# An attention loop on one core: the row of reciprocals goes through the shared PSUM bank ahead of the value products, and the shift is made by a two-scalar operation

## The reference

```python
def _L0_attn_ref(hidden_size, Wq_c, bq_c, Wq_up, bq_up, Wkv_c, bkv_c, Wkv_up, bkv_up, Wo, bo):
    ...
    scores = jnp.einsum('bhqd,bhkd->bhqk', q, k) / np.sqrt(Q_HEAD)
    attn = jax.nn.softmax(scores, axis=-1)
    o = jnp.einsum('bhqk,bhkv->bhqv', attn, v)
    out = jnp.einsum('bhsv,Hv->bsH', o, Wo) + bo
    return out
...
x = x + _L0_attn_ref(_layernorm(x, axis=-1), ...)
x = x + _L0_ffn_ref(_layernorm(x, axis=-1), ...)
```

## Time and profile before

| | |
|---|---|
| median of 3 runs | 1855.05 us |
| the profiled execution | 1852.05 us, its span 1850.2 us |
| PE busy | 1650.0 us, 89% |
| DVE busy | 1618.4 us, 87% |
| ACT busy | 1416.3 us, 77% |
| POOL busy | 969.6 us, 52% |
| granted TensorE clock | 0.994 of full speed |

### The profile page before, as it was taken

One profiled execution on the slowest core, in us unless ns is written; L12 is line 12 of the kernel. 1 busy time (PEld: TensorE's weight loads), 2 busy tenths in 40 slices (PEclk: granted clock), 3 DMA queues, 4 the chain that ended last, 5 costly groups with the idle time before them and its releaser, 6 DMA issues. The chain is left out here.

```text
span 1850.2 us, 23339 instructions
## 1 busy us (share of the span) xinstructions
PE 1650.0 (89%) x7316; PEld 753.7 (41%) x7316; DVE 1618.4 (87%) x2088; ACT 1416.3 (77%) x1979; POOL 969.6 (52%) x1355
## 2 busy tenths in 40 slices
PE   7988988998989889889989898898898988988799
PEld 6733333333333333333333333333333333333344
DVE  6679999999989999999989999999989999999565
ACT  5578888888878888888878888888878888888422
POOL 3246556565555565565555655555546555555320
PEclk9999999999999999999999999999999999999999
DMA  6599999999999999999999999999999999999611
GB/s 211 179 188 191 187 190 186 188 190 183 190 173 185 186 190 188 190 183 191 183 176 190 186 188 190 183 190 183 188 175 189 188 189 185 190 187 182 150 44 48
DMA packets 1092405, 330.84 MB, mean 179 GB/s; under 512 B 1070336, under 2 KB 1076768, under 8 KB 1092288
## 3 DMA queue, kind: packets, MB, share of 16 engines
q1 hardware_dynamic: 1080128, 296.22, 87.1%
q0 software_dynamic: 12160, 33.18, 6.6%
HBM read 50.39 MB, written 10.49 MB: 33 GB/s over the span
## 5 line engine op out<-in xcount | busy, mean ns | idle before, releaser
L969 DVE TENSOR_REDUCE mx<-S 128x1 f32<-128x1024 f32 x512 | 621.1, 1213 | 123.9 <-PE S L830 123.9
L925 ACT ACTIVATE S<-S,shift,unscale 128x1024 f32<-128x1024 f32 x512 | 602.0, 1176 | 158.0 <-DVE shift L975 145.9
L961 DVE TENSOR_TENSOR halves<-S,halves 128x1024 f16<-128x1024 f32 x512 | 621.6, 1214 | 2.6 <-ACT halves L934 2.6
L934 ACT ACTIVATE halves<-S 128x1024 f16<-128x1024 f32 x512 | 523.8, 1023 | 16.1
L828 PE MATMUL S<-kvTH,qeH 128*128 128x512 f16 x1024 | 392.2, 383 | 97.6 <-POOL qeL L740 93.2
L753 POOL TENSOR_TENSOR diagonal<-ident,recip 128x512 f32<-128x512 f32 x128 | 131.7, 1029 | 493.0 <-PE O L862 480.1
L830 PE MATMUL S<-kvTH,qeL 128*128 128x512 f16 x1024 | 388.1, 379 | 0.0
L829 PE MATMUL S<-kvTL,qeH 128*128 128x512 f16 x1024 | 388.1, 379 | 0.0
L840 PE MATMUL O<-PT,kvn 128*128 128x512 f16 x1024 | 243.6, 381 | 0.0
L975 DVE SCALAR_TENSOR_TENSOR shift<-mx,unscale,c_lift 128x1 f32<-128x1 f32 x512 | 225.8, 441 | 18.2
L828 PEld LDWEIGHTS S<-kvTH,qeH 128*128 128x128 f16 x1024 | 99.4, 97 | 332.1 <-POOL qeL L740 146.9
(11 more groups left out here) (263 smaller groups left out, 2018.6 us busy)
## 6 DMA issues: line engine op xcount, KB each, us to landing
weff<-weff_scratch POOLq DMA_DIRECT2D x126, 192.0 KB, 4.6
wv<-in_wv POOLq DMA_DIRECT2D x128, 64.0 KB, 3.1
PT<-halves SPq DMA_TRANSPOSE x512, 5.0
raw<-in_raw SPq DMA_DIRECT2D x8, 772.0 KB, 6.7
weff_scratch<-w_split SPq DMA_DIRECT2D x8, 768.0 KB, 5.2
x<-in_x SPq DMA_DIRECT2D x4, 1024.0 KB, 6.8
x_all<-in_x SPq DMA_DIRECT2D x3, 1024.0 KB, 5.6
out<-y SPq DMA_DIRECT2D x3, 1024.0 KB, 4.3
```

Of the source, the lines that this page charges most:

```text
L925: nc.scalar.activation(S[:, t % SLOTS, :], S[:, t % SLOTS, :], ACT.Exp, bias=shift[:, col:col + 1], scale=keep["unscale"][:, 0:1], accum_o ...
L934: nc.scalar.activation(halves[u][:, 0, :], S[:, t % SLOTS, :], ACT.Copy).then_inc(high_out, 1)
L961: v.tensor_tensor(halves[u][:, 1, :], S[:, t % SLOTS, :], halves[u][:, 0, :], ALU.subtract).then_inc(low_out, 1)
L969: v.reduce_max(mx[:, col:col + 1], S[:, t % SLOTS, :], AX.X).then_inc(max_ready, 1)
```

## The change

Two things are changed.

First, the order in which bank `O` is used. The row is now made from the reciprocals of step g-1 instead of g-2, at a later place in step g (behind `scores(2)`, after the next queries have been copied out), and ScalarE copies it to SBUF (`recip_row`, two buffers). The value products of step g+1 then go into `O` and stay there until `normalized` reads them straight from PSUM, with the row as its other operand from SBUF. The copy `osum` is gone. `next_queries` moves from behind `scores(2)` to in front of it.

Second, the shift. The maximum is written negated, and the shift is a `tensor_scalar` with one tensor operand (`mx`) and two per-partition scalars (`unscale`, `c_lift`) where it was a `scalar_tensor_tensor` with two tensor operands and one scalar.

```diff
                 def values():
-                    if on:
-                        pe.wait_ge(q_copied, g + 1)
+                    if g >= 3:
+                        pe.wait_ge(onorm_ready, g - 2)
+                    pe.wait_ge(row_out, g - 1)
...
-                def repeat_row(out):
-                    pe.wait_ge(diagonal_ready, g - 1)
+                def repeat_row(k, out):
+                    pe.wait_ge(ones_set, 3)
+                    pe.wait_ge(diagonal_ready, k + 1)
                     mm(out, square[:], diagonal[:].rearrange("p u c -> p (u c)"), start=True, stop=True).then_inc(row_filled, 1)
...
                 if on:
                     scores(1)
-                    if g >= 2:
-                        pe.wait_ge(ones_set, 3)
-                        pe.wait_ge(o_out, g - 1)
-                        repeat_row(O[:])
-                    scores(2)
                     if exists(g + 1):
                         next_queries()
+                    scores(2)
+                    if exists(g - 1):
+                        if exists(g + 1):
+                            pe.wait_ge(q_copied, g + 2)
+                        elif g >= 2:
+                            pe.wait_ge(onorm_ready, g - 1)
+                        repeat_row(g - 1, O[:])
...
-                if exists(g - 2):
+                def copy_row(out):
+                    act.wait_ge(row_filled, g)
                     if g >= 3:
                         act.wait_ge(onorm_ready, g - 2)
-                    act.wait_ge(pv_done, g - 1)
-                    nc.scalar.activation(osum[:], O[:], ACT.Copy).then_inc(o_out, 1)
+                    nc.scalar.activation(row[1 - par][:], out, ACT.Copy).then_inc(row_out, 1)
+
                 if exists(g):
                     for u in range(UN):
                         if u == 2 and exists(g + 1):
                             copy_q(g + 1, (h + 1) % NH, 1 - par)
+                        if u == 3 and exists(g - 1):
+                            copy_row(O[:])
                         exp(u)
                         high(u)
...
-                    v.reduce_max(mx[:, col:col + 1], S[:, t % SLOTS, :], AX.X).then_inc(max_ready, 1)
+                    v.reduce_max(mx[:, col:col + 1], S[:, t % SLOTS, :], AX.X, negate=True).then_inc(max_ready, 1)
...
-                    v.scalar_tensor_tensor(out=shift[:, col:col + 1], in0=mx[:, col:col + 1], scalar=keep["unscale"][:, 0:1],
-                                           in1=keep["c_lift"][:, at], op0=ALU.mult, op1=ALU.subtract,
-                                           reverse1=True).then_inc(shift_ready, 1)
+                    v.tensor_scalar(shift[:, col:col + 1], mx[:, col:col + 1], keep["unscale"][:, 0:1],
+                                    keep["c_lift"][:, at], ALU.mult, ALU.add).then_inc(shift_ready, 1)
...
-                def normalized(row):
-                    dve.wait_ge(o_out, g - 1)
-                    dve.wait_ge(row_filled, g - 1)
+                def normalized():
+                    dve.wait_ge(pv_done, g - 1)
+                    dve.wait_ge(row_out, g - 1)
                     if g >= 3:
                         dve.wait_ge(onorm_low, g - 2)
-                    v.tensor_tensor(onorm[:], osum[:], row, ALU.mult).then_inc(onorm_ready, 1)
+                    v.tensor_tensor(onorm[:], O[:], row[par][:], ALU.mult).then_inc(onorm_ready, 1)
```

More of the change, by code:

```diff
@@ L620, in attention @@
         wvs = sb("wv_scaled", [KVL, VH])
-        onorm, onormH, onormL, osum = (keep[n] for n in ("onorm", "onormH", "onormL", "osum"))
+        onorm, onormH, onormL = (keep[n] for n in ("onorm", "onormH", "onormL"))
+        row = [sb(f"recip_row{i}", [P, BLK]) for i in range(2)]
         diagonal, square = sb("diagonal", [P, UN, P]), sb("ones_square", [P, P])
@@ L637, in attention @@
                  "wv_split", "onorm_high", "onorm_low", "ffn_in", "row_ready", "bo_added", "projected0", "summed0",
-                 "stats0", "std0_done", "rstd0_done", "sign_ready", "q_filled", "q_high", "q_copied", "q_low", "o_out")
+                 "stats0", "std0_done", "rstd0_done", "sign_ready", "q_filled", "q_high", "q_copied", "q_low", "row_out")
         (bv_in, ones_set, scores_ready, max_ready, shift_ready, probs_ready, high_out, low_out,
@@ L641, in attention @@
          wv_split, onorm_high, onorm_low, ffn_in, row_ready, bo_added, projected0, summed0,
-         stats0, std0_done, rstd0_done, sign_ready, q_filled, q_high, q_copied, q_low, o_out) = (sem(n) for n in names)
+         stats0, std0_done, rstd0_done, sign_ready, q_filled, q_high, q_copied, q_low, row_out) = (sem(n) for n in names)
         ident = keep["ident"]
@@ L873, in body @@
                     project_tile(UN - 1)
-                if g == NG + 1:
-                    repeat_row(S[:, 2, 0:BLK])
                 if exists(g - 2):
@@ L879, in body @@
                 if g == NG:
-                    pe.wait_ge(ones_set, 3)
-                    repeat_row(S[:, 2, BLK:2 * BLK])
+                    repeat_row(g - 1, S[:, 2, 0:BLK])
                 if on:
                     scores(1)
-                    if g >= 2:
-                        pe.wait_ge(ones_set, 3)
-                        pe.wait_ge(o_out, g - 1)
-                        repeat_row(O[:])
-                    scores(2)
                     if exists(g + 1):
                         next_queries()
+                    scores(2)
[5 more added lines that the diff above has]
+                        repeat_row(g - 1, O[:])
                     if h == 2 and b:
@@ L947, in body @@
                 if g == NG:
+                    copy_row(S[:, 2, 0:BLK])
                     act.wait_ge(row_ready, 1)
@@ L968, in maximum, with shifted @@
                     dve.wait_ge(scores_ready, t + 1)
-                    v.reduce_max(mx[:, col:col + 1], S[:, t % SLOTS, :], AX.X).then_inc(max_ready, 1)
-                def negated(u):
+                    v.reduce_max(mx[:, col:col + 1], S[:, t % SLOTS, :], AX.X, negate=True).then_inc(max_ready, 1)
+                def shifted(u):
                     col = par * UN + u
@@ L1020, in body @@
                         maximum(u)
-                        negated(u)
+                        shifted(u)
                         if u == 1 and g >= 2:
-                            normalized(O[:])
+                            normalized()
                         if UN * g + u:
@@ L1039, in body @@
                     reciprocals()
-                    normalized(S[:, 2, BLK:2 * BLK])
+                    normalized()
                     add_projection(UN - 1)
@@ L1053, in body @@
                 if g == NG + 1:
-                    normalized(S[:, 2, 0:BLK])
+                    normalized()
                     dve.wait_ge(wv_done, NG - 1)
@@ L1288, in layer @@
             "sign": sb("sign", [P, 2]), "factor": sb("factor", [P, 1]), "xn2": sb("xn2", [P, UN, HID]),
-            "osum": sb("osum", [P, BLK]), "onorm": sb("onorm", [P, BLK]),
+            "onorm": sb("onorm", [P, BLK]),
             "onormH": sb("onormH", [P, BLK], F32R), "onormL": sb("onormL", [KVL, BLK], F32R),
```

## The result

The changed kernel takes 2068.78 us in the median of 4 runs (2065.32 to 2072.69), the kernel before 1854.88 us (4 runs). The ratio is 1.1145, with a 95% interval from 1.1106 to 1.1185. The sign was forecast, the size was not: 118 us more were predicted, 214 us were measured, and the time lies outside the range of 1925 to 2020 us.

A forecast was written before the change was run, and what follows sets the result against it. A dependence loop through PE, ACT, POOL and DVE was taken as the bound (12.67 us). With stall and copy wait the step became 13.64: 125 steps +121, tail -2, median +3, forecast 1973 us, range 1925 to 2020.

The forecast's parts named there:

- The circle: Dependence loop onorm, queries, qeL, scores, maximum, shift of tile 1, back to onorm: sets the old step of 12.67 us.
- The stall: PE idle between scores(1) and the queries, waiting for maximum, shift and onorm: 2.32 us in each step.
- The wait for the copied row: PE's values wait for ACT's row copy, queued behind exponential and high of tile 2: adds 0.09 us per step.
- `scores(3)` and `output`: PE's work after the row in the step laid out: 2.36 us together, ending at 8.13.
- The lower end of the range: Queries' first matmul loses 0.3 us start-up and no copy wait: step 13.25 us, +73, total 1927 us.
- The step that failed: Sum over the loop: 0.97 us more in each of 125 steps, +121 us.
- a clock below 1.00 in the loop: Sign of being wrong: TensorE's granted clock in the loop below 1.00, which is 2.4 GHz.
- rival (d): TensorE's clock falls after the new stall, 1 to 2 us in each step: 2095 to 2220 us; 7 in 100.
- My own price: Cost of TensorE's clock falling 1 to 2 us per affected step: 12 to 25 us if one step in ten.
- (a): DVE was the true bound; freeing it gives steps of 11.8 us, about 1746 us; 4 in 100.
- (b): Stall before the queries is covered, nothing changes; PE would have to save 0.87 of 2.32 us; 2 in 100.
- (c): DVE's new shift stays blocked by POOL: stall 0.55 us longer, step 14.2 us, about 2042 us; 4 in 100.

The follow-up runs named there:

- e2: The kernel before with the new shift alone (negated maximum, two scalars), order untouched: 1795.16 us, ratio 0.9644.
- e3: The changed kernel with eight extra unused matmuls between scores(1) and the wait of the queries: 1987.83 us, ratio 1.0684.
- e4: The changed kernel with onorm made in front of the maximum of tile 1 on DVE: 1976.55 us, ratio 1.0631.
- e5: The changed kernel with onorm before tile 1's maximum and ACT's query copy ahead of tile 1's exponential: 1721.7 us, ratio 0.9275.
- e8: The changed kernel with onorm before tile 1's maximum, the query copy ahead of tile 1's exponential, and the old shift: 1801.82 us, ratio 0.9702.
- e1: The changed kernel with the old shift (two tensor operands), so the new order alone: 2043.81 us, ratio 1.0968.

## Why the prediction was right and wrong

**The circle** was right: the shift of tile 1, shortened by 0.50 us alone, made the step 0.49 us shorter (e2).

**The stall** was right in place, cause and size: 2.32 us predicted, 2.40 measured. The parts are 0.21 to the maximum, 1.26 to the shift, 0.19 to `onorm` (0.13 predicted; the new shift takes 0.27 and not 0.22), 0.68 and 0.06.

**The wait for the copied row** was right in kind and too small. `scores(0)` at 1016.04 should hand over to the values 1.31 later; they start 1.56 later, at 1017.60, 0.10 after the copy has ended. So 0.25 us, where 0.09 was predicted. The chain on DVE and ACT had gathered 0.12 us until the copy starts, and its end reached PE 0.04 later than I took. The stall and this wait are 0.24 us more than predicted; `scores(3)` and `output` gave 0.08 back (2.28 for 2.36). So the step is 13.79 against 13.64, worth 19 us. The lower end of the range let the queries lose 0.3 us of start-up, a term that no row shows: they took 1.27 us behind the stall (1.28 before). And 1971 plus the 3 us of the median is 1974, not 1973.

**The step that failed** is the sum, "13.64 - 12.67 = 0.97 us per step ... 125 of them: +121 us". It takes all steps to be equal, at a granted clock of 1.00, and so puts the cost of the clock at nothing. 55 intervals of 127 were longer, at a granted clock of 0.89: they had 81.6 us too much. The prediction named a clock below 1.00 in the loop as a sign of being wrong, and the sign came. I had the mechanism as rival (d) and gave it 7 in 100, on one row in which a wait of 2.35 us had left the clock alone. What I weighed was a fall in most steps or none; a fall in somewhat less than half of them, at 1.5 us each, lay between the forecast and the rival, and in no range. My own price, "in one step of ten 12 to 25 us", gives 53 to 108 us at the 55 of 127 that fell, and holds the 82 measured: what was mis-sized is how often. With the clock held by fillers the kernel takes 1988 us (e3), inside the range and 15 us above the forecast, by the 19 us of the step.

Of the clock the Trainium skill (TensorE: Matmul & The Clock Gate, HAM oscillation) says that a kernel with idle gaps in each round can pay the fall in each round; here it was paid in 4 rounds of 10. The gaps that the section describes are longer, DMA waits of some 3 to 5 us; the 2.4 us here were enough in part of the rounds.

**The rivals.** (a) DVE as the bound: excluded by e2. (b) A covered stall: the order as changed does not cover it, but two further moves do (e4 and e5). (c) A shift that stays blocked: all 512 shifts of the new form take between 271 and 276 ns in the changed kernel, and 272 to 276 ns in e2, where GpSimd's `diagonal` is still in their way. The contention through a two-port mode of `tensor_scalar`, which the Trainium skill (SBUF — State Buffer, Who interferes with whom) names as possible, doesn't appear in this 128 x 1 form. Its other rule, that a VectorE instruction with two SBUF inputs contends with a GpSimd instruction that reads SBUF, was borne out before and in e8 (0.77 and 0.94 us where 0.22 is undisturbed).

## What to carry to other kernels

When an instruction that waits is moved forward in an engine's queue, look at what stood between it and the last thing it depends on: that was its cover. Here the change freed the shared bank for the value products but left `onorm` and the copy of the queries at their old places on the other two engines, and these two lines decide between 1.11 times and 0.93 times the old time. A stall on TensorE in each step can have a second price, its clock: here 82 us for stalls of 2.4 us, next to 142 us for the longer step. Filling the stall with matmuls whose output nobody uses tells in one run how large that is. And a small operation with two SBUF tensors costs what GpSimd happens to be doing, so it has to be measured again in each order.

## What the runs showed of the hardware

- A fall of the clock after a stall does not depend on the length of the stall alone. PE waits shown with 2.22 us in each step gave falls in 56 of 127 intervals, 2.20 us (at another place in the step) in 14, 1.79 us in 6, 0.50 us in none (the last two intervals of the loop, where other gaps stand, are left out). In about half of the falls of the changed kernel the clock was still at 1.00 after the stall and at 0.50 some 1.5 us later; in the other half it was at 0.50 from the end of the stall on. The falls are regular: pairs in three or four steps in the changed kernel, mostly pairs in five in e1, one in eleven in e4. That points to a rhythm of its own against which the steps run, rather than to chance, and e1, with a step 0.04 us shorter and 18 us less lost, fits it. No run here tests it, and why 2.20 us in e4 gave so many fewer falls than 2.22 us stays open.
- A shift of 128 x 1 with two scalars takes 273 ns, with two tensors 220 ns when nothing blocks it. The new form is slower by 50 ns and was never blocked: it wins where the old one meets GpSimd on the circle (before against e2, e8 against e5), and not in the changed order itself (e1).
